# Deeper scatters of rank 0, low halves spread over the blocks, and the last root on GpSimd, in a layer of a state-space model and a mixture of experts

## The reference

```
decays = sigmoid(x @ Wd + bd);  inj = x @ Wi + bi
h[t] = decays[t] * h[t-1] + inj[t]                      # scan over 2048 tokens
x = layernorm(x + (layernorm(h) * gamma + beta + x))
gate = x @ Wg.T + routing_bias;  top 4 of 8 experts;  softmax over those 4
out = swiglu(x, Ws1, Ws2, Ws3)                          # the shared expert
    + sum over the chosen experts e of weight_e * swiglu(x, W1[e], W2[e], W3[e])
x = layernorm(x + out)
```

## Time and profile before

| | us |
|---|---|
| median of three runs | 1046.53 |
| the runs | 1039.69, 1046.53, 1047.74 |
| the profiled execution | 1038.96 |
| its span, first to last instruction | 1035.8 |
| TensorE busy in the span | 988.5 |
| VectorE busy | 590.0 |
| GpSimd busy | 531.6 |
| ScalarE busy | 525.4 |

### The profile page before, as it was taken

The page is one execution under the profiler, slowest core; times in us unless marked ns, Lnnn a source line. Parts: engine busy times, 40 slices in busy tenths (PEclk is TensorE's granted clock), DMA queues, the critical chain, the costliest instruction groups (busy, mean ns, idle before and its releaser), DMA issues.

```text
span 1035.8 us, 27298 instructions
## 1 busy us (share of the span) xinstructions
PE 988.5 (95%) x8630; PEld 840.9 (81%) x8630; DVE 590.0 (57%) x1680; ACT 525.4 (51%) x1367; POOL 531.6 (51%) x501
## 2 busy tenths in 40 slices
PE   9997989979999999999999999999999999999986
PEld 4556867867888888888878888888888888887875
DVE  3998896545545454544545445545455454444786
ACT  3675644434555455545545554545454554554465
POOL 3554054358233234843648007066888861884870
PEclk9997999989999999999999999999999999999999
DMA  8946132443532333253243423228864872885792
GB/s 249 224 114 167 22 84 85 141 92 84 176 97 83 95 98 103 83 174 99 69 145 84 108 48 101 70 54 173 127 98 78 127 111 52 122 123 85 95 163 92
DMA packets 167891, 113.83 MB, mean 110 GB/s; under 512 B 113436, under 2 KB 160031, under 8 KB 166688
## 3 DMA queue, kind: packets, MB, share of 16 engines
q0 software_dynamic: 30480, 59.41, 27.0%
q1 hardware_dynamic: 114960, 32.07, 15.4%
q10 hardware_dynamic: 22400, 21.76, 6.1%
HBM read 47.09 MB, written 40.96 MB: 85 GB/s over the span
## 4 chain that ended last, share of the span: by engine, by line
PE 43%; DMA 28%; POOL 12%; issue 7%; DVE 6%; ACT 1%; SPq 0%; ACTq 0%; POOLq 0%; DVEq 0%
PE psA L996 28%; DMA rows_by_place<-y_rows,place 25%; PE psB L1023 10%; POOL y_sum L702 4%; POOL rows_by_place L658 3%; POOL work L588 2%; PE psA L947 1%; POOL work L581 1%; POOL stage L582 1%; DMA y_sum<-rows_by_place,place 1%; PE psC L978 1%; PE psB L1026 1%; DVE g_lo L1406 1%; DMA rows_by_place<-zeros,pad_at 1%; DVE work L1202 1%
## 5 line engine op out<-in xcount | busy, mean ns | idle before, releaser
L816 ACT ACTIVATE sil<-psA 128x256 f32<-128x256 f32 (+1 forms) x510 | 187.1, 373 | 289.0 <-PE psA L996 214.9
L1396 DVE SCALAR_TENSOR_TENSOR g<-psA,sil 128x256 f32<-128x256 f32 (+1 forms) x178 | 73.5, 414 | 315.3 <-ACT sil L816 288.2
L658 POOL DMA_INDIRECT rows_by_place<-y_rows,place x128 | 127.5, 996 | 225.7 <-DMA rows_by_place<-y_rows,place 178.3
L702 POOL DMA_INDIRECT y_sum<-rows_by_place,place x128 | 198.6, 1552 | 84.6 <-DMA rows_by_place<-eb 39.3
L996 PE MATMUL psA<-xb_odd,work 128*128 128x256 f16 x2112 | 235.8, 273 | 1.8 <-issue 1.2
L996 PE MATMUL psA<-xb,work 128*128 128x256 f16 x2046 | 230.7, 274 | 6.9 <-issue 4.5
L996 PEld LDWEIGHTS psA<-xb_odd,work 128*128 128x128 f16 x2112 | 206.1, 98 | 26.9 <-issue 3.2
L996 PEld LDWEIGHTS psA<-xb,work 128*128 128x128 f16 x2046 | 200.6, 98 | 33.1 <-issue 9.0
L1023 PE MATMUL psB<-work,g_hi 128*128 128x256 f16 x1320 | 221.1, 273 | 4.1 <-DVE g_lo L1406 3.6
L1396 DVE SCALAR_TENSOR_TENSOR psC<-psA,sil 128x256 f32<-128x256 f32 (+1 forms) x332 | 140.1, 422 | 82.4 <-ACT sil L816 69.6
L1023 PE MATMUL psB<-work,g_lo 128*128 128x256 f16 x660 | 179.9, 273 | 0.0
(11 more groups left out here) (159 smaller groups left out, 842.0 us busy)
## 6 DMA issues: line engine op xcount, KB each, us to landing
stage<-wpack POOLq DMA_DIRECT2D x9, 2176.0 KB, 9.1
rows_by_place<-eb ACTq DMA_DIRECT2D x63, 256.0 KB
work<-half_beta SPq DMA_DIRECT2D x8, 512.0 KB, 4.9
work<-x_tok POOLq DMA_DIRECT2D x8, 512.0 KB, 6.0
work<-xT SPq DMA_DIRECT2D x7, 512.0 KB, 4.5
rows_by_place<-y_rows,place POOLq DMA_INDIRECT x128, 2.5
y_sum<-rows_by_place,place POOLq DMA_INDIRECT x128
out<-y_sum ACTq DMA_DIRECT2D x4, 512.0 KB
```

The source lines that it names most:

```text
L658: pool.indirect_dma_start(out=xs, out_offset=bass.IndirectOffsetOnAxis(ap=place[:, k, n:n + 1], axis=0), in_=y_rows[:, n, :], in_offset=No ...
L702: pool.indirect_dma_start(out=y_sum[:, n, :], out_offset=None, in_=xs, in_offset=bass.IndirectOffsetOnAxis(ap=place[:, k, n:n + 1], axis=0 ...
L816: act.activation(sil[r0:r0 + n, c % SLOTS, 0:T], psA[0:n, c % HVS, 0:T], ACT.Silu, scale=1.0 / (XS * WS)).then_inc(silu_ready, 1)
L1396: dve.scalar_tensor_tensor(gated_rows(g, c, 0, n, T), src, 1.0 / (XS * WS), sil[r0:r0 + n, c % SLOTS, 0:T], ALU.mult, ALU.mult).then_inc(g ...
```

## The change

Four things are changed:

- Rank 0 is scattered by a function of its own, `scatter_first`: scatter n waits for scatter n - 3, over three semaphores, in all 32. The padding rows of expert 0 are written after the 31st scatter, ahead of the 32nd.
- SP calls `expert_row` ahead of its waits.
- The low halves of steps 4, 6, 1, 3, 5 and 7 are made inside blocks 2 to 7, one step per block, each step in two pieces of two tiles (`low_half`), after the gated product of a chunk. The `first_low` pieces 0 to 5, which were in blocks 2, 3 and 4, go to blocks 4 to 8: one each in 4 to 7, two in 8. ScalarE's `first_high` pieces move with them. `pads` goes from behind block 2 into block 7.
- The last lot's root is made by GpSimd, by the four instructions that make the one of the lot before; VectorE's part of the last scaling becomes `last_groups`.

```diff
-        scattered = [[sem(f"scattered{k}_{i}") for i in range(2)] for k in range(K)]
+        scattered = [[sem(f"scattered{k}_{i}") for i in range(FLIGHT if k == 0 else 2)] for k in range(K)]
...
+                row = expert_row(sp, e)
                 if e < K:
-                    for i in range(2):
-                        sp.wait_ge(scattered[e][i], 16 * NT // 2)
+                    for i, landed in enumerate(scattered[e]):
+                        sp.wait_ge(landed, 16 * len(range(i, NT, len(scattered[e]))))
                 sp.wait_ge(pads_written[e], 16)
-                expert_blocks(sp, e % 2, expert_row(sp, e), load_rows)
+                expert_blocks(sp, e % 2, row, load_rows)
...
-            def scatter(k, overlapped=0, beside=None):
+            def scatter_first(beside):
 
                 for n in range(NT):
-                    if k == 0 and n % JT == 0:
+                    if n % JT == 0:
                         pool.wait_ge(y_low_ready, low_rank(B * (n % (NT // B) // JT) + n // (NT // B)))
-                    if n > 1 and (n < overlapped or overlapped and n % 2 == 0):
-                        pool.wait_ge(scattered[k][n % 2], 16 * (n // 2))
-                    if n > 0 and (n >= overlapped and (n % 2 == 0 or not overlapped)):
+                    if n >= FLIGHT:
+                        pool.wait_ge(scattered[0][n % FLIGHT], 16 * (n // FLIGHT))
+                    pool.indirect_dma_start(
+                        out=xs, out_offset=bass.IndirectOffsetOnAxis(ap=place[:, 0, n:n + 1], axis=0),
+                        in_=y_rows[:, n, :], in_offset=None).then_inc(scattered[0][n % FLIGHT], 16)
+                    beside(n)
+
+            def scatter(k, beside=None):
+
+                for n in range(NT):
+                    if n:
                         pool.wait_ge(scattered[k][(n - 1) % 2], 16 * ((n - 1) // 2 + 1))
...
-            scatter(0, 20)
-            pool.wait_ge(pad_places_ready, 1)
-            pad_rows(0)
+            def first_pads(n):
+                if n == NT - JB:
+                    pool.wait_ge(pad_places_ready, 1)
+                    pad_rows(0)
+
+            scatter_first(first_pads)
             pool.wait_ge(first_low_ready, len(pieces) + len(MIXED))
             fetch(2)
             pool.wait_ge(blocks_ready, 1)
             pool.wait_ge(pads_written[0], 16)
-            scatter(1, 0, convert_beside(1, 5, 20))
+            scatter(1, convert_beside(1, 5, 20))
...
-            pool.wait_ge(pool_moments_ready, 1)
...
+            for n, lot in enumerate((POOL_LOT, len(LOTS) - 1)):
+                m = JB * len(FINISH[LOTS[lot]])
+                nmv_, nv_, nr_, na_, nb_ = (row[lot % 2] for row in (nmv, nv, nr, na, nb))
+                assert m <= 2 * JT
+                pool.wait_ge(pool_moments_ready, n + 1)
...
             for g in range(2, S1):
-                ffn_block(g, beside=lambda c: first_high(2 * (g - 2) + (c == 3)) if g < 5 and c in (1, 3) else None)
+                if 4 <= g < 8:
+                    ffn_block(g, beside=lambda c: first_high(g - 4) if c == 3 else None)
+                elif g == 8:
+                    ffn_block(g, beside=lambda c: first_high(4 + (c == 3)) if c in (1, 3) else None)
+                else:
+                    ffn_block(g)
...
+            def low_half(s, h):
+
+                g0 = tok(s) // P + JB * h
+                dve.wait_ge(y_high_ready, s + 1)
+                ins = dve.scalar_tensor_tensor(y_hl[:, g0:g0 + JB, 1, :], y[:, g0:g0 + JB, :], XS,
+                                               y_hl[:, g0:g0 + JB, 0, :], ALU.mult, ALU.subtract)
+                if h:
+                    ins.then_inc(y_low_ready, 1)
...
                 for c in range(NC):
                     gated(c)
-                    if c == 1 and beside:
+                    if c == at and beside:
                         beside()
-                    if c in (3, 5) and later is not None:
-                        first_low(later + (c == 5))
+                    if rows_at and c in rows_at:
+                        low_half(*rows_at[c])
+                    if first_lows and c in first_lows:
+                        first_low(first_lows[c])
                     if c:
                         low(c - 1)
                 low(NC - 1)
...
-            ffn_block(2, beside=weigh, later=0)
-            low_rows(4)
-            pads()
-            low_rows(6)
+            ffn_block(2, beside=weigh, rows_at={3: (4, 0), 4: (4, 1)})
             add_shared(2, 2)
-            ffn_block(3, beside=sizes, later=2)
-            low_rows(1)
-            low_rows(3)
+            ffn_block(3, beside=sizes, rows_at={3: (6, 0), 4: (6, 1)})
             add_shared(3, 3)
-            ffn_block(4, later=4)
-            low_rows(5)
-            low_rows(7)
+            ffn_block(4, first_lows={5: 0}, rows_at={2: (1, 0), 3: (1, 1)})
             add_shared(4, 4)
-            for g in range(5, S1):
-                ffn_block(g)
-                add_shared(g, g)
+            ffn_block(5, first_lows={5: 1}, rows_at={2: (3, 0), 3: (3, 1)})
+            add_shared(5, 5)
+            ffn_block(6, first_lows={5: 2}, rows_at={2: (5, 0), 3: (5, 1)})
+            add_shared(6, 6)
+            ffn_block(7, beside=pads, first_lows={5: 3}, rows_at={2: (7, 0), 3: (7, 1)})
+            add_shared(7, 7)
+            ffn_block(8, first_lows={3: 4, 5: 5})
+            add_shared(8, 8)
...
+            def last_groups(lot, pairs):
+
+                groups = [y[:, q * JB + j, :] for q in pairs for j in range(JB)]
+                m = len(groups)
+                dve.wait_ge(pool_lot_ready, 2)
+                for j in range(m // 2, m):
+                    dve.tensor_scalar(groups[j], groups[j], nr[lot % 2][:, j:j + 1], nb[lot % 2][:, j:j + 1],
+                                      ALU.mult, ALU.add).then_inc(last_normed, 1)
...
-            t.add(moments(len(LOTS) - 1, FINISH[S2 - 1]))
-            inverse(len(LOTS) - 1, FINISH[S2 - 1])
+            moments(len(LOTS) - 1, FINISH[S2 - 1]).then_inc(pool_moments_ready, 1)
+            last_groups(len(LOTS) - 1, FINISH[S2 - 1])
```

More of the change, by code:

```diff
@@ L81, in build @@
     GS = 3
+    FLIGHT = 3
     FIELD_BITS = 7
@@ L145, in build @@
         assert 2 * SETW <= 10
-        neg_half = sb("neg_half", [P, JT], F32)
+        neg_half = sb("neg_half", [P, 2 * JT], F32)
         low_row = sb("low_row", [P, 1], F32)
@@ L552, in rstd1 @@
                 t.wait()
-                pool.tensor_tensor(rs1[b][:, :], ve[:, :], neg_half[:, :], ALU.pow).then_inc(rstd1_ready, 1)
+                pool.tensor_tensor(rs1[b][:, :], ve[:, :], neg_half[:, 0:JT], ALU.pow).then_inc(rstd1_ready, 1)
             def rstd2(s):
@@ L564, in rstd2 @@
                 t.wait()
-                t.add(pool.tensor_tensor(rs2[b][:, :], ve[:, :], neg_half[:, :], ALU.pow))
+                t.add(pool.tensor_tensor(rs2[b][:, :], ve[:, :], neg_half[:, 0:JT], ALU.pow))
                 t.wait()
@@ L689, in _ @@
             pool.wait_ge(pads_written[2], 16)
-            scatter(3, 0, convert_beside(2, 1, 16))
+            scatter(3, convert_beside(2, 1, 16))
             pool.wait_ge(pads_written[2], 16)
@@ L732, in _ @@
             t = Tally(pool, pool_lot_steps)
-            m = JB * len(FINISH[LOTS[POOL_LOT]])
-            nmv_, nv_, nr_, na_, nb_ = (n[POOL_LOT % 2] for n in (nmv, nv, nr, na, nb))
-            assert m <= JT
-            pool.wait_ge(pool_moments_ready, 1)
-            t.add(pool.tensor_scalar(nv_[:, 0:m], nmv_[:, 0:m, 1], 1.0, LN_EPS, ALU.mult, ALU.add))
-            t.add(pool.tensor_scalar(na_[:, 0:m], nmv_[:, 0:m, 0], -1.0, 1.0, ALU.mult, ALU.mult))
-            t.wait()
-            t.add(pool.tensor_tensor(nr_[:, 0:m], nv_[:, 0:m], neg_half[:, 0:m], ALU.pow))
-            t.wait()
-            pool.tensor_tensor(nb_[:, 0:m], na_[:, 0:m], nr_[:, 0:m], ALU.mult).then_inc(pool_lot_ready, 1)
+            for n, lot in enumerate((POOL_LOT, len(LOTS) - 1)):
[3 more added lines that the diff above has]
+                pool.wait_ge(pool_moments_ready, n + 1)
+                t.add(pool.tensor_scalar(nv_[:, 0:m], nmv_[:, 0:m, 1], 1.0, LN_EPS, ALU.mult, ALU.add))
+                t.add(pool.tensor_scalar(na_[:, 0:m], nmv_[:, 0:m, 0], -1.0, 1.0, ALU.mult, ALU.mult))
+                t.wait()
+                t.add(pool.tensor_tensor(nr_[:, 0:m], nv_[:, 0:m], neg_half[:, 0:m], ALU.pow))
+                t.wait()
+                pool.tensor_tensor(nb_[:, 0:m], na_[:, 0:m], nr_[:, 0:m], ALU.mult).then_inc(pool_lot_ready, 1)
         @block.scalar
@@ L885, in norm_groups @@
             def norm_groups(lot, part, parts):
-                if part == 0 and lot == POOL_LOT:
-                    act.wait_ge(pool_lot_ready, 1)
+                if part == 0 and lot >= POOL_LOT:
+                    act.wait_ge(pool_lot_ready, lot - POOL_LOT + 1)
                 elif part == 0:
-                    act.wait_ge(lot_ready, lot + 1 - (lot > POOL_LOT))
```

(10 more changed lines are left out.)

## The result

| | before | after |
|---|---|---|
| median of 20 runs each, us | 1044.30 | 1051.01 |
| lowest and highest | 1036.97, 1050.36 | 1041.36, 1060.26 |
| ratio after to before, 95% interval | | 1.0071 [1.0049, 1.0093] |

The change costs 6.7 us of median (7.4 by the ratio). A second set of runs beside the last experiments gave 1049.86 against 1044.59, 1.0052 [1.0022, 1.0082].

What follows compares the result with a forecast made beforehand. GpSimd's serial scatters of ranks 1 to 3, tied with TensorE at expert 3, were taken as the bound. +3.9 (chain) + 2.4 (clock) - 0.75 (root) = +5.55 on 1038.96, 1044.5; on the median 1050, 8 in 10 from 1041 to 1058.

Steps and rivals of the forecast that it cites:

- The fetch: Expert 1's weights, behind the last `first_low` in block 8: issued at 204.5 instead of 199.81.
- The first scatter of rank 1: Behind the fetch on GpSimd's queue: landing at 213.25, 8.75 after the fetch, so the serial program starts 3.9 us later.
- Low halves by pieces: Blocks 2 to 8: 128x512 pieces at 0.62 us; block 8 starts 4.5 earlier, TensorE gains 3.5 by its end.
- TensorE's idleness at expert 3: Ahead of expert 3: TensorE ready at 522.1, starting at 530.1, so idle for 8 us; its 3.5 gain is lost.
- The clock: After the idleness at expert 3: granted clock 0.50, costing 2.4 us, with ends 0 and 4.5.
- The root: Last lot's tail, moved to GpSimd: 1.8 us instead of 2.56, a gain of 0.75, ends 0.3 and 0.9.
- SP's registers: Expert 0, SP reading registers ahead of its wait: gains nothing, under 1 us if the rows came late.
- The sum and the median: Whole kernel: +5.55 us on the profiled 1038.96 gives 1044.5; on the median 1049.7 or 1052.1, stated as 1050.
- Rival 1: At expert 3: serial program not late, TensorE keeps 3.5 and the tail 0.75, giving 1042.3; chance 0.15.
- Rival 2: At expert 3: delay half made up, chain +2, clock never lower than before, 1047 to 1048; chance 0.13.
- Rival 3: Blocks 5 to 8: stalls of 2 us each shift the whole chain by 8 more, giving 1058; chance 0.12.
- Rival 4: Rank 0: three in flight does nothing, as scatters 16 to 31 wait for low halves; part of the forecast, no separate chance.

Runs made afterwards that it cites:

- the first profile: Profile of the changed kernel with nothing further altered, from an execution of 1060.08 us.
- the second profile: The changed kernel profiled once more with nothing further altered: execution 1047.85 us, span 1046.1.
- the kernel with the rows first: Changed kernel, two in flight in ranks 1-3, pieces and conversions at earlier chunks, TensorE registers beside block 8, fetch waiting for expert 0's first rows: 1028.43 us, 0.9856.

## Why the prediction held, step by step

**What bounds the kernel: right, and shown.** Taking away GpSimd's serial program as the limit, with the fetch left late, takes 10 to 12 us from the changed kernel; delaying the fetch in the kernel before costs as much as the change (with a collision of its own in it). The rank-0 scatters of the change, alone, are a gain.

**The fetch: right in cause, short in size.** Said +4.7 (204.5), came +5.5 over the first stage. One term was short. A block with a `first_low` at chunk 5 is 0.33 us and more over 10.70 and not 0.15, so blocks 4 to 6 took 33.3 and not 32.6 (block 8 started 69.9 behind block 2, said 69.2). The reading of the earlier trace rows had it right, an overdraft of about 0.3; the sum then took half of it without a reason. The way from block 8's start to the end of the copies is 205.59 + 0.47 - 195.88 = 10.2, as said.

**The first scatter of rank 1: wrong term.** I took 8.75 us from the fetch to its landing, by the second fetch of the trace, because the pads were long landed. It took 9.5: the next scatter went at 216.09, 0.27 behind it, 9.46 after 206.36 (and 9.85 in the first profile); the 9.56 of the earlier trace rows would have been the right row. The program thus starts 5.4 later instead of 3.9. The Trainium skill's 2.0 us plus bytes over 436 GB/s (DMA: Bandwidth & Descriptors, Anatomy of one DMA — SWDGE (gpsimd) path), from which I had an estimate of 7.1 for the fetch, is not what any run here shows: this one fetch took 8.3 to 10.4 in the thirteen profiles.

**Low halves by pieces.** 128x512 took 0.68 (said 0.62), the blocks 14.15, 11.2, 11.1 on average, 11.2 and some 11.9 (said 14.3, 11.2, 10.85, 11.1, 11.7). The other row of this step was right too: scatters of rank 0 waited for low halves in the first profile for 6.11, 6.59 and 5.77 us each, whatever the depth. What I had missed is expert 0's rows: in pairs they are loaded behind the fetch, and TensorE waits 8.9 us for them.

**TensorE's idleness at expert 3: right place, mis-sized.** Said 8, came 12.93 and 19.57. It would have been ready at 533.66 - 12.93 = 520.73. From expert 0 to the fourth of its blocks TensorE took 247.31 - 212.55 = 34.76 where it took 252.45 - 213.77 = 38.68 before, with short waits for VectorE; so it gained 3.9 more that I had not counted, and 2.2 ahead of expert 0 instead of 3.5. The 4.9 by which the idleness is over 8 are in two parts: 2.4 of them are TensorE's gain, which never reaches the end, and 2.5 are the program's, 6.4 later over the first stage instead of 3.9, which does. I had named 5 to 10 us as the sign; the sign was exceeded, the other ones (fetch at 203 to 207, second scatter at 212 to 217, clock at 0.50) came as named.

**The clock.** Said 0.50 and 2.4 us, came 9.91 for the pass (+2.5). The 2.4 was taken against 7.20, where the earlier trace rows have 7.37 for such a pass; it came out right all the same. The program's own 0.9 and a second drop at block 9 (+1.5) were not in the sum.

**The root.** Said 0.75, came 0.95. **SP's registers.** Said nothing; TensorE's wait ahead of expert 0 is still put to issue, 4.72.

**The sum and the median.** Said +5.55 against one profile; the second profile has 10.3 - 1.0 = 9.3 over its first stage. On the medians the change costs 6.7 (or 5.3). The two needn't agree: the median of before already holds some 4 us of the chain (two in flight in ranks 1 to 3 take them out) that its profile, 5.3 below the median, did not show. I had left that open as "a likely place". It is part of the distance to the median; the spread stays without the chain, much of it is in the first stage, and what lengthens that stage I haven't found. That 1050 lies so near 1051.01 is in part luck: it was added to a median of 1046.53 from three runs, which twenty runs put at 1044.30, and the step that it holds, 3.5, is about half of what came.

Rival 1 (not slower) is out: it needed the fetch by 196.3. Rival 2 (half made up) is out in the profiles, though the short run with the late fetch shows that the program can take 3.5 us less than in the profile of before. Rival 3 (stalls of 2 us in the blocks) is out: 0.3 to 0.6. Rival 4 stands as far as the fetch goes; for expert 0's rows the depth may matter.

## What to carry to other kernels

A queue shown busy for half the span can set the end: look for the place where a busier engine waits for it with almost no slack, and price every move by what it does to that queue's first instruction. Work that is spread to smooth one engine must not include what another engine's long serial program waits for; here the conversions had to stay early, or the program had to be shortened first. After each repair look at what the same wait is put down to: registers, then row weights, then nothing, and only the last step paid. And look at what a moved transfer now meets: the late fetch also held up expert 0's row weights.

## What the runs showed of the hardware

- **A small load issued behind a large fetch on another queue lands after it.** The fetch is 2176 KB on GpSimd's queue, the load 8 KB on SP's. SP's timeline of the kernel with the rows first, whose fetch goes out at 204.06 and lands at 204.06 + 9.8 = 213.9, then TensorE's:

```profile
201.56 0.44 SPq L501 DMA_DIRECT2D row_weights<-rows_by_place  x1
...
207.96 0.39 SPq L501 DMA_DIRECT2D row_weights<-rows_by_place  x1
```

```profile
217.43 7.38 PE L1016 MATMUL psA<-xb,work 128*128 128x256 f16 x66 [1.13 <-DMA row_weights<-rows_by_place]
```

  The first load landed after 1.90 us, the second, 3.9 us behind the fetch, after 9.34. Loads 1.0, 1.8 and 3.6 us behind the fetch made TensorE wait 6.71, 8.91 and 7.45 us in three kernels and landed about 1 us after it; loads that went out within 0.03 us of it, in two profiles, had landed 2.5 us later. All go into memory of the core. I did not vary the sizes, and GpSimd's next scatters stand behind the fetch in every one, so the fetch's own share isn't separated from theirs.
- **TensorE's clock can fall after less than 2 us of idleness.** All thirteen profiles idle for 1.67 to 1.72 us ahead of block 9 of the shared expert. TensorE's timelines there, first before, then the kernel with the late fetch:

```profile
945.89 7.38 PE L996 MATMUL psA<-xb,wshared 128*128 128x256 f16 x66 [1.67 <-SPq L450]
```

```profile
948.01 8.91 PE L997 MATMUL psA<-xb,wshared 128*128 128x256 f16 x66 [1.69 <-SPq L450]
```

  Windows of 1 us of the latter have a clock of 1.00 at 946, 0.89 at 947 and 0.50 from 948. Six profiles lost 1.5 to 1.7 us so (8.89 to 9.04): both of the changed kernel, the late fetch, the two kernels that differ from before and after by the pairs alone, and the last one with the registers moved. The other seven, the kernel before among them, lost nothing (7.38). What decides isn't known; it is worth up to 1.7 us of difference between two profiles.
- **Scatters in flight together go out every 1.27 us**, 0.96 of the instruction and 0.30 of issue, as long as none waits for a landing, against the 2.7 of one at a time.
